# A gated window-attention and router kernel: the loop over pairs of batches written out, and another order of the work within a step

## The reference

```
xn  = layernorm(x) over the 2048 columns
q   = Wq xn + bq ; k = Wk ctx + bk ; v = Wv ctx + bv        (256x256 weights)
att = softmax over a window of 16 columns of q.k / sqrt(32), 8 heads of 32 rows; times v
x1  = x + tanh(g_xattn) * (Wo att + bo)
h   = layernorm(x1) ; logits = h Wr^T + rbias (64 experts) ; scores = softmax(logits)
w   = the 8 largest scores, the others zero
out = x1 + tanh(g_ffn) * (h * sum(w) + w expert_bias)
```

## Time and profile before

| | before |
|---|---|
| median of 3 runs | 1618.49 us (1618.11 to 1618.87) |
| the profiled execution | 1618.16 us, span 1616.3 us |
| granted clock of TensorE, mean | 0.97 |
| busy: PE | 1485.2 us, 92% of the span |
| busy: PEld / DVE / ACT / POOL | 1220.9 / 1271.2 / 1148.2 / 1147.7 us |
| instructions | 68923 |
| DMA | 210.75 MB, 130 GB/s mean |

### The profile page before, as it was taken

How to read it: one execution, slowest core, us unless ns; L and a number is a source line. 1 busy time by engine, 2 the same in 40 slices (tenths; PEclk the granted TensorE clock), 3 DMA queues, 4 the chain that set the end, 5 groups by cost and what they waited for, 6 DMA issues and landing times.

```text
span 1616.3 us, 68923 instructions
## 1 busy us (share of the span) xinstructions
PE 1485.2 (92%) x28162; PEld 1220.9 (76%) x28162; DVE 1271.2 (79%) x2970; ACT 1148.2 (71%) x2009; POOL 1147.7 (71%) x1110
## 2 busy tenths in 40 slices
PE   2599999999899998999989998999989999989986
PEld 1477888888688886887878886887878888778764
DVE  4378888888688786888868897788868888798863
ACT  3478877777677776877767786777767777767752
POOL 2587777687587776777767776777757777767761
PEclk8799999999999999999999999999999999999996
DMA  6354455445445554454545545445545555534332
GB/s 196 99 153 110 125 162 137 127 146 150 112 128 138 143 144 131 106 174 129 134 123 154 140 109 172 107 133 150 127 133 131 134 139 149 139 82 123 68 76 84
DMA packets 365609, 210.75 MB, mean 130 GB/s; under 512 B 294496, under 2 KB 295520, under 8 KB 361056
## 3 DMA queue, kind: packets, MB, share of 16 engines
q1 hardware_dynamic: 365280, 206.14, 47.8%
HBM read 136.88 MB, written 33.55 MB: 105 GB/s over the span
## 4 chain that ended last, share of the span: by engine, by line
PE 51%; DVE 19%; issue 13%; POOL 11%; ACT 3%; DMA 2%; SPq 1%; DVEq 0%; POOLq 0%; ACTq 0%
PE ps_j L1122 18%; PE ps_a L1146 8%; PE ps_s L1181 7%; PE ps_s L1122 6%; PE ps_r L1223 4%; DVE prob_t L905 2%; POOL x L492 2%; POOL score L497 2%; POOL att_lo L473 2%; PE ps_a L1200 2%; POOL x_lo L484 2%; PE ps_t L1163 2%; PE ps_s L1176 1%; PE ps_a L1201 1%; POOL c_lo L478 1%
## 5 line engine op out<-in xcount | busy, mean ns | idle before, releaser
L497 POOL TENSOR_TENSOR score<-score,p_inv 128x384 f32<-128x384 f32 x256 | 221.2, 864 | 115.0 <-DVE p_inv L899 114.2
L504 POOL TENSOR_TENSOR prob<-score,prob 128x384 f16<-128x384 f32 x256 | 265.9, 1039 | 38.3 <-ACT prob L656 37.1
L1146 PE MATMUL ps_a<-prob_t,v_diag 128*128 128x64 f16 (+1 forms) x6528 | 218.5, 193 | 46.0 <-issue 30.5
L1146 PEld LDWEIGHTS ps_a<-prob_t,v_diag 128*128 128x128 f16 x6528 | 205.6, 99 | 70.5 <-issue 48.0
L1181 PEld LDWEIGHTS ps_s<-kv_win,q_col 32*32 32x32 f32 x16384 | 194.4, 105 | 63.3 <-issue 63.3
L478 POOL TENSOR_TENSOR c_lo<-c_in,c_hi 128x1024 fp32r<-128x1024 f32 x64 | 152.1, 2377 | 126.2 <-ACT c_hi L630 126.2
L1181 PE MATMUL ps_s<-kv_win,q_col 32*32 32x48 f32 x16384 | 230.9, 203 | 9.0 <-issue 8.9
L905 DVE STREAM_TRANSPOSE prob_t<-prob 128x512 f32<-128x512 f32 x256 | 176.1, 698 | 74.9 <-POOL prob L504 48.5
L473 POOL TENSOR_TENSOR att_lo<-att,att_hi 128x512 fp32r<-128x512 f32 x128 | 162.5, 1274 | 80.3 <-ACT att_hi L616 79.8
L1122 PE MATMUL ps_j<-c_hi,wkv_hi 128*128 128x512 f32 x512 | 170.8, 415 | 43.2 <-POOL c_lo L478 33.3
L884 DVE TENSOR_REDUCE neg_max<-ps_s 128x8 f32<-128x384 f32 x256 | 139.8, 546 | 68.9 <-PE ps_s L1181 68.3
(11 more groups left out here) (149 smaller groups left out, 3325.2 us busy)
## 6 DMA issues: line engine op xcount, KB each, us to landing
v_diag<-v_turn SPq DMA_DIRECT2D x512, 68.0 KB, 2.8
c_in<-ctx_dram SPq DMA_DIRECT2D x64, 512.0 KB, 4.3
x_in<-x_dram SPq DMA_DIRECT2D x64, 512.0 KB, 5.3
x_res<-x_dram SPq DMA_DIRECT2D x64, 512.0 KB, 4.3
out_dram<-x SPq DMA_DIRECT2D x32, 1024.0 KB, 7.2
c_sq<-ctx_dram SPq DMA_DIRECT2D x60, 512.0 KB, 5.0
x<-ctx_dram SPq DMA_DIRECT2D x4, 512.0 KB, 6.0
x<-experts_dram SPq DMA_DIRECT2D x2, 512.0 KB, 10.3
```

Source lines behind the costliest of these rows:

```text
L497: pool.tensor_tensor(score[:, u], score[:, u], p_inv[:, u, :].unsqueeze(2).to_broadcast([P, HALF, KEYS]), ALU.mult).then_inc(pm_rdy, 1)
L504: pool.tensor_tensor(part(prob[:, u % 2], 1)[:, :, 0:KEYS], score[:, u], part(prob[:, u % 2], 0)[:, :, 0:KEYS], ALU.subtract).then_inc(pl_ ...
L1146: ins = pe.matmul(ps_a[g][:, q0:q1], part(v_diag[:, g, j], kv), part(prob_t[:, g, lo:hi], kp), start=(j == 0 and n == 0), stop=(j == NB), ...
```

## The change

The loop is gone: `walk` calls `step` for all steps with whole numbers, and the register arithmetic on SP goes with it. Within a step every engine but SP gets another order. No instruction's shape changes.

```diff
-        def walk(eng, step):
-            for c in (2, 3):
-                step(-1, c, 1)
-            for b in range(2):
-                for c in range(NCH):
-                    step(b, c, b % 2)
-            with eng.Fori(2, B - 3, 2) as b:
-                for c in range(NCH):
-                    step(b, c, 0)
-                for c in range(NCH):
-                    step(b + 1, c, 1)
-            for b in range(B - 2, B + 1):
-                for c in range(NCH):
-                    step(b, c, b % 2)
+        def walk(step):
+            for n in range(-2, N + NCH):
+                step(n // NCH, n % NCH, (n // NCH) % 2)
...
                     need(pe, x1_rdy[g], nth(b, c, off))
-                    need(pe, xt_rdy[1 - g], nth(b, c, -2))
+                    need(pe, xt_rdy[1 - g], nth(b, c, off - (1 - g)))
```

More of the change, by code:

```diff
@@ L273, in live @@
         def live(b, c, off):
-            return not isinstance(b, int) or 0 <= NCH * b + c + off < N
+            return 0 <= NCH * b + c + off < N
         def final(b, g, j):
@@ L678, in step @@
                 now, before = live(b, c, 0), live(b, c, -1)
[L679 to L682, removed]
+                if live(b, c, 1):
+                    keys_high(1, 1)
+                    keys_high(0, 1)
                 if live(b, c, 2):
                     context_high()
-                if now:
-                    queries_high(1, 0)
                 if live(b, c, -2):
@@ L690, in step @@
                     attention(0)
+                if now:
+                    queries_high(1, 0)
+                if before:
+                    attention_high(0)
+                    attention(1)
+                    attention_high(1)
+                if c == 2 and seq(b - 1):
+                    need(act, wt_mm, b)
+                    act.activation(wd_both[:], ps_t[:, 0:G * P].rearrange("e (g p) -> e g p", g=G), ACT.Copy).then_inc(wt_rdy, 1)
+                    act.activation(wd_one[:], ps_t[0:E + 2, G * P:2 * G * P].rearrange("e (g p) -> e g p", g=G),
+                                   ACT.Copy).then_inc(wt_rdy, 1)
+                if live(b, c, 1):
+                    centre()
+                if now:
+                    exponent(0)
+                if live(b, c, 1):
+                    x_high()
                 if c == 2 and seq(b + 1) and now:
@@ L937, in step @@
                     need(dve, x_ld[ch], (b + db + 1) * 16)
+                    stats_in(0, ch)
                     stats_in(1, ch)
-                    stats_in(0, ch)
-                if now:
-                    largest(0)
-                    values_turn(0)
-                    values_turn(1)
-                    shift(0)
                 if stats and c == 3:
@@ L948, in step @@
                 if now:
+                    values_turn(0)
+                    values_turn(1)
+                    largest(0)
+                    shift(0)
+                if routing:
+                    router_logits(b, 0)
+                if now:
+                    largest(1)
+                if routing:
+                    router_logits(b, 1)
+                if now:
                     total(0)
-                    largest(1)
-                    invert(0)
-                if c == 2 and seq(b + 1) and now:
-                    weights_low(b + 1, 1 - par)
+                if routing:
+                    router_logits(b, 2)
                 if now:
                     shift(1)
+                if routing:
+                    router_logits(b, 3)
                 if finishing(b, c):
@@ L997, in step @@
                 if now:
+                    largest(3)
+                    shift(3)
+                if before:
+                    stats_x1(0)
+                if now:
+                    total(2)
+                if live(b, c, 2):
+                    values_low(1)
+                if now:
+                    total(3)
+                    invert(2)
+                    invert(3)
                     turn(0, 0)
@@ L1257, in step @@
                     queries(1, 0)
-                if live(b, c, -2):
-                    rows(1, -2)
-                if now:
-                    scores(0)
                 if before:
@@ L1273, in step @@
                     ins.then_inc(wt_mm, 1)
+                if now:
+                    scores(0)
+                if live(b, c, -2):
+                    router()
+                if now:
+                    scores(1)
                 if c == 1 and seq(b + 1) and now:
@@ L1311, in step @@
                     ins.then_inc(sum_mm, 1)
-            walk(pe, step)
+            walk(step)
 def kernel(**inputs):
```

225 lines of the change are left out of this document (95 added, 130 removed).

## The result

| | before | after |
|---|---|---|
| median of 4 runs each | 1618.67 us (1618.11 to 1618.87) | 1660.61 us (1659.71 to 1661.3) |
| ratio | | 1.0259, 95% interval 1.0242 to 1.0277 |
| span profiled, mean granted clock | 1616.3 us, 0.970 | 1658.6 us, 0.955 |

The account below looks back on a forecast made before the run. PE was taken as the bound, busy 1190.9 of 1239.6 us. Fourteen batches of 97.3 us (1362), 148.6 before them, 89.2 for batch 15, 40.7 at the end and 1.9 around the span gave 1642 us, range 1617 to 1661.

Parts of the forecast that it names:

- Sign and mechanism: Whole kernel: slower, chance 0.61; POOL instructions hold DVE, so PE waits in c = 1 and c = 2.
- The wait of c = 1: PE waits for `output_bias(1)` behind the held second norm and ACT's logit exponentials: 3.6 us, bounds 2.6 to 4.1.
- the walk: Going through the four other engines' queues with trace durations, t = 0 at `attend(0)`, to time what PE wants.
- The wait of c = 2: PE waits for wd_cat because c_lo and `attention_low` hold DVE's `router_weights`: 2.7 us, bounds 1.9 to 3.5.
- Rival C: Both waits also lower PE's clock, a 1.1 us slow block each: 31 us more, 1673 us; chance 0.08.
- The loop: Removing five back edges, each 5.2 us idle plus 1.1 of slow `attend(0)`, gains 31.5 us, bounds 26 to 36.
- small stalls: Small fetch stalls of PE, 14 us over 15 batches, kept in the new kernel as 0.9 us a batch.
- The sum: A batch is 89.7 + 0.9 + 0.4 + 3.6 + 2.7 = 97.3 us; the kernel 1642 us.
- small stalls and transitions: Per batch: 0.9 us of fetch stalls, and 0.4 for more changes between kinds of PE work.
- The 1.1 us that I took off c = 3: Step c = 3: about 1.1 us of 24.3 taken as small waits, leaving an estimated 23.2 dense.
- A (dense): PE dense everywhere, collisions shorter or in slack: 91.0 us a batch, 1550 us; chance 0.17.
- B (only ACT's queue): Only ACT's queue bites, router weights come through before c_lo: 93.5 us a batch, 1589 us; chance 0.17.

Follow-up runs that it names:

- clo_late: The kernel after, with POOL's `context_low` moved behind `attention_low(0)` and `attention_low(1)`: 1593.6 us, 0.9843 of the kernel before.
- both: The kernel after with the edits of `logits_late` and `clo_late` together: 1560.24 us, 0.9645 of the kernel before.
- logits_late: The kernel after, with ACT's four exponentials of the logits in c = 1 moved behind `output_bias`: 1671.07 us, 1.0324 of the kernel before.
- unrolled: The kernel before with its loop written out, old order kept: 1564.38 us, 0.9681 of the kernel before.
- loop_of_four: The kernel before with a loop body of four batches, two back edges instead of five: 1593.24 us, 0.9867 of the kernel before.
- order_in_loop: The kernel after with the old loop over pairs of batches put back, new order kept: 1694.98 us, 1.0492 of the kernel before.
- best: `both` plus DVE's `shift(1)` right behind `largest(1)` in c = 1: 1546.95 us, 0.9569 of the kernel before.

## Why the prediction was right, and where its terms were off

**Sign and mechanism: right.** Where the forecast had two waits a batch, for `output_bias` in c = 1 and for wd_cat in c = 2, they stand, in each of batches 1 to 14, and the chain that leads to them is the one walked through: `inverse_root` ends at 7.4 us (forecast 6.3 to 8.0), `shift(0)` at 10.9 (9.9 to 11.5). The logits' exponentials start at 15.2 (13.4 to 14.9), and `output_bias(1)` is done at 17.7 (15.8 to 17.3). `clo_late` and `both` show by removal that these are the causes: with `context_low` moved, the held instructions fall to 153 to 223 ns.

**The wait of c = 1: 3.6 forecast, 3.95 measured** (3.30 + 0.65). Both ends of it came later than I had them: the chain by the hold of neg_top under x_lo (1.61 us at 1364.38), which the walk did not have, and PE, which wants `values(1)` at 14.5 and not 13.7, since `scores(3)` had to wait.

**The wait of c = 2: 2.7 forecast, 1.65 measured.** `turn(3)` was through at 1.1 us, not 2.2, so the first two-input operations passed ahead of c_lo. What was held is L1073, a cast with one input, that I had let pass. The Trainium skill (SBUF — State Buffer, Who interferes with whom) has this too: `copy`, `cast` and `tensor_scalar` can enter a mode that takes both ports, and then contend. I had gone by its rule on two inputs only. The trace agrees at 2.43 us for the cast (1381.10), 1.61 for neg_top.

**The clock: the term that failed.** Rival C, that the waits lower the clock as well, had 0.08, because one wait of 2.39 us had not lowered it. It came true in c = 1 of every batch, at 1.5 to 2.4 us, 2.05 in the mean, 29 us over 14 batches. C had priced 31 for both waits, at 1.1 each, since that was the price of `attend(0)` alone behind a back edge; the slow stretch there goes on for some us more (1.05 us at 435.66). And the trace of before had two waits of nearly the forecast's length, both of 3.06 us and both with the lower clock behind them: one at 1553.02, with a mean of 0.66 over the next 5 us, and this one at the end of batch 15:

```profile
1575.58 2.74 PE L1146 MATMUL ps_a<-prob_t,v_diag 128*128 128x32 f16 x51 [3.06 <-DVE prob_t L905]
```

A single row in which something did not happen was poor evidence: `clo_late` shows a wait of 1.85 us followed by either level, `logits_late` one of 3.1. In c = 2 of the kernel after, behind 1.65 us, it came once in fourteen steps (28.7 us, the other thirteen 25.6 to 25.7).

**The loop: undersized.** 31.5 forecast, 52 with the old order, 34 to 38 with the new. A back edge is worth about 7.2 us, not 6.3, and its error is the slow clock behind the gap: 2.2 us and not the 1.1 of `attend(0)`. The small stalls, which I kept as 0.9 us a batch, went with the loop too: "issue" is 3.9 us in all in `unrolled` and 3.4 in the kernel after. The Trainium skill's figure of about 108 ns for a compare-and-branch (Advanced Engine Details and Errata, Control Flow Timing) would put `loop_of_four` and the kernel before 0.3 us apart, an estimate from it for three edges; they differ by 21.7 us.

**The sum.** A batch was to be 97.3 us and is about 98.85, by steps (forecast, then measured): c = 0 21.3, 21.4; c = 1 25.2, 27.6; c = 2 26.3, 25.65; c = 3 23.2, 24.2; small stalls and transitions 1.3, none. In c = 3 most of the 1.0 is a wait that the walk did not have, 0.6 us of `rows(0)` for POOL's `residual(0)`; `clo_late` removes it too (23.4 where PE has no "issue" gap). The 1.1 us that I took off c = 3 for small waits was no term of the loop's either: `unrolled` keeps 24.3. Fourteen times 1.55 are 22 us, the one slow c = 2 is 3 more, and the end 1. Against them, batch 1 begins at 140.5 us and not at 148.6: the two waits of PE for the first c_lo are shorter. One row of the waits of before and one of after:

```profile
PE ps_j L1122 <- POOL c_lo L478: 33.3, 2, 24.7
```

```profile
PE ps_j L1104 <- POOL c_lo L455: 23.9, 2, 17.9
```

That is 8 us of gain that I had not looked for. It is the order's: batch 1 begins at 141.3 us in `order_in_loop` and at 146.6 in `unrolled`. 1642 + 22 + 3 + 1 - 8 = 1660. So 35 us of terms that erred the other way (18 of small stalls and transitions, 9 in c = 2, 8 at the start) stand against the clock's 29 and some 24 of others, and that the time came out so near was in part luck. It lies at the very top of the forecast's own range (1661).

**The rivals.** A (dense) would have been right with two calls moved: `both`, at 1560, is what it described, and `best` beats its 1550. B (only ACT's queue) had the weights pass ahead of c_lo; that needed c_lo moved, and `clo_late` at 1594 is close to its 1589.

What stays open: what makes the same wait end in one level of the clock or the other from batch to batch; what the small stalls in the loop are, some 15 us, since the profile shows nothing that PE waits for; and why they vanish with the new order inside the loop.

## What to carry to other kernels

Before moving a large GpSimd instruction earlier, list which VectorE instructions start inside it and can take the shared port (two SBUF inputs, or casts and tensor_scalar), and follow the first queue that waits for each of them: here one call in another place was worth 67 us. A wait of PE has two prices, its length and what the clock does behind it; read the granted clock behind the wait in every batch, not in one, and test with useless matmuls in its place. When a fix of one wait brings nothing, look for the next wait down the same queue before dropping the fix: `logits_late` alone cost 10 us, and on top of `clo_late` it gave 33.

## What the runs showed of the hardware that I had not expected

- A back edge of a loop with a body of two batches (some 8300 instructions over all engines, an eighth of 66658) cost about 7.2 us (5 to 9): 5 us in which PE issues nothing, and 3 to 6 us behind it at a granted clock of 0.50 (before). Being in the loop cost another 15 us or so.
- Behind a wait of 1.85 us the granted clock stayed at 1.00 in five steps and fell to 0.50 in ten; behind one of 2.9 to 3.1 us (`logits_late`) it stayed in four and fell in ten. Once down it stayed down for 3.2 to 3.5 us in `clo_late` and for 9 us or more in `logits_late`.
- A VectorE cast of 128x128 took 2.43 us and a tensor_scalar on 128x2 1.61 us, each to the end of the GpSimd instruction that it had started in; free, L1070 on 128x2 takes 0.17.
- Sixteen useless matmuls a batch made a kernel 43 us faster.
